# Cross-attention in a decoder layer: the first context block of the next batch is rounded two steps earlier

## The reference, cut to what matters

```
x = x + _L0_attn_ref(_layernorm(x), W_K, W_Q, W_V, W_O)
x = x + _L0_xattn_ref(_layernorm(x), ctx_2048, Wq, Wk, Wv)
x = x + _L0_ffn_ref(_layernorm(x), ...)          # mixture of experts

def _L0_xattn_ref(x, context, Wq, Wk, Wv):       # x (8,112,512), context (8,375,512)
    q = x @ Wq.T
    k_raw = context @ Wk.T
    v_raw = context @ Wv.T
    ...                                          # 32 heads of 16; k, v interleaved
    q = _rmsnorm(q); k = _rmsnorm(k)
    attn = softmax(q k^T * 0.25)
    return attn @ v
```

## Time and profile before

| | |
|---|---|
| median of 3 runs | 905.11 us (905.03 to 905.36) |
| the profiled execution | 905.82 us, its span 904.0 us |
| PE busy | 887.2 us |
| DVE busy | 599.0 us |
| ACT busy | 464.1 us |
| POOL busy | 203.5 us |

### The profile page before, as it was taken

The page is one execution under the profiler, slowest core; times in us unless marked ns, Lnnn a source line. Parts: engine busy times, 40 slices in busy tenths (PEclk is TensorE's granted clock), DMA queues, the critical chain, the costliest instruction groups (busy, mean ns, idle before and its releaser), DMA issues.

```text
span 904.0 us, 17919 instructions
## 1 busy us (share of the span) xinstructions
PE 887.2 (98%) x7088; PEld 777.9 (86%) x7088; DVE 599.0 (66%) x1304; ACT 464.1 (51%) x1119; POOL 203.5 (23%) x147
## 2 busy tenths in 40 slices
PE   8999999999999999999999999999999999999995
PEld 8998989898989898777787787777877898999994
DVE  7886575757575635765655655646557878888883
ACT  5533334343434344647666667566675336656551
POOL 0143232333333225201101101011000621132233
PEclk9999999999999999999999999999999999999998
DMA  6221232323212115140101001000043687989973
GB/s 225 64 94 41 91 126 94 123 94 123 95 53 96 40 47 180 35 129 30 55 12 36 14 24 36 13 24 14 1 147 140 230 310 295 364 280 308 294 203 46
DMA packets 42195, 104.56 MB, mean 116 GB/s; under 512 B 8208, under 2 KB 18560, under 8 KB 40192
## 3 DMA queue, kind: packets, MB, share of 16 engines
q1 hardware_dynamic: 37808, 94.23, 30.5%
q0 software_dynamic: 4304, 9.19, 5.0%
HBM read 75.57 MB, written 18.65 MB: 104 GB/s over the span
## 4 chain that ended last, share of the span: by engine, by line
PE 90%; DVE 2%; ACT 2%; POOL 2%; DMA 2%; issue 1%; SPq 0%; DVEq 0%
PE bank L595 23%; PE bank L596 23%; PE bank L597 23%; PE bank L852 5%; PE bank L869 5%; PE bank L695 3%; PE bank L671 2%; DMA ctx_f<-ctx 1%; PE bank L711 1%; PE bank L812 1%; PE bank L683 1%; PE bank L981 1%; PE bank L879 1%; POOL wkv_lo L2330 1%; PE bank L989 1%
## 5 line engine op out<-in xcount | busy, mean ns | idle before, releaser
L1380 ACT ACTIVATE ee<-bank 125x448 f32<-125x448 f32 x192 | 90.8, 546 | 15.0 <-PE bank L852 15.0
L1628 DVE TENSOR_TENSOR E_lo<-F,E_hi 128x940 fp32r<-128x940 f32 (+3 forms) x62 | 80.9, 1321 | 2.0 <-ACT E_hi L1147 1.9
L595 PE MATMUL bank<-wkv_hi,ctx_hi 128*125 128x512 f32 x192 | 79.9, 416 | 0.4 <-DVE kn L1905 0.4
L2330 POOL TENSOR_TENSOR ctx_lo<-ctx_f,ctx_hi 128x500 fp32r<-128x500 f32 x24 | 30.5, 1275 | 209.0 <-ACT ctx_hi L1147 209.0
L596 PE MATMUL bank<-wkv_hi,ctx_lo 128*125 128x512 f32 x192 | 76.1, 396 | 0.0
L597 PE MATMUL bank<-wkv_lo,ctx_hi 128*125 128x512 f32 x192 | 75.7, 394 | 0.0
L1147 ACT ACTIVATE E_hi<-F 128x940 fp32r<-128x940 f32 (+3 forms) x62 | 67.9, 1140 | 7.4 <-PE bank L597 3.6
L2330 POOL TENSOR_TENSOR wqk_lo<-wqk_f,wqk_hi 128x1024 fp32r<-128x1024 f32 x14 | 35.1, 2505 | 155.1 <-ACT wqk_hi L1147 155.1
L2440 POOL DMA_INDIRECT out<-yg,meta x21 | 39.1, 1864 | 127.7 <-DMA out<-yg,meta 71.7
L595 PE MATMUL bank<-wv_hi,xT_hi 128*128 128x256 f32 x224 | 63.4, 283 | 0.1
L597 PE MATMUL bank<-wv_lo,xT_hi 128*128 128x256 f32 x224 | 62.6, 279 | 0.0
(11 more groups left out here) (411 smaller groups left out, 2581.1 us busy)
## 6 DMA issues: line engine op xcount, KB each, us to landing
F<-wexp SPq DMA_DIRECT2D x14, 1408.0 KB, 7.6
F<-wexp SPq DMA_DIRECT2D x14, 768.0 KB, 6.9
wqk_f<-wqk SPq DMA_DIRECT2D x16, 512.0 KB, 4.3
ctx_f<-ctx SPq DMA_DIRECT2D x24, 250.0 KB, 2.7
slots<-zt SPq DMA_DIRECT2D x3, 1799.0 KB, 8.1
xg<-slots SPq DMA_DIRECT2D x21, 256.0 KB, 7.2
wv_f<-wv SPq DMA_DIRECT2D x8, 512.0 KB, 5.7
wo_f<-wo SPq DMA_DIRECT2D x8, 512.0 KB, 3.4
```

The lines of the kernel that those rows point to most:

```text
L595: e.matmul(out, a[0], b[0], start=first, stop=False)
L1380: e.activation(ee[(4 * n + r) % 8][:, :], SX[r][0:MS, 0:4 * T], ACT.Exp, scale=0.25).then_inc(*x_exped.did((n, r)))
L1628: return e.tensor_tensor(out, src, high.bitcast(F32), ALU.subtract)
L2330: return e.tensor_tensor(out, src, high.bitcast(F32), ALU.subtract)
```

## The change

The steps in which context blocks are rounded are 6b - 1, 6b + 2 and 6b + 3 instead of 6b + 1, 6b + 2 and 6b + 3. Block 3b + 3 is thus rounded in the last item's step of the batch before, for b = 1 to 6; the other blocks stay where they were. The high half on ACT, the low half on POOL and with it the release of a later load move.

```
-        ctx_step = {6 * b + i + 1: [3 * b + 3 + i] for b in range(NB - 1) for i in range(3) if b or i}
+        ctx_step = {6 * b + (-1, 2, 3)[i]: [3 * b + 3 + i] for b in range(NB - 1) for i in range(3) if b or i}
```

## The result

| | before | after |
|---|---|---|
| median | 905.28 us (15 runs, 904.78 to 907.33) | 907.73 us (15 runs, 906.45 to 909.58) |
| the profiled execution | 905.82 us, span 904.0 | 907.50 us, span 905.7 |

The ratio is 1.0026, interval 1.0018 to 1.0034: the changed kernel is slower by 2.45 us, where 4.9 us less were forecast. The time lies 5.8 us above the upper end of the range, 901.9.

The account below looks back on a forecast made before the run. PE (TensorE) was taken to bound the kernel, busy 98% of the span, with six stalls for kT. Removing them wins 4.95 us, other parts costing nothing: 905.11 - 4.95 = 900.2 us, range 899.5 to 901.9.

Parts of the forecast that it names:

- the six waits for kT: Cross-attention, line 711: PE waits 3.4 us in all for DVE's kT copy, late behind xn; the change removes them.
- Points 2 and 3: Third item's steps: xn falls from 1.43 to 0.55, the kT wait goes, steps last 6.19; 4.95 us won over six.
- Point 4: Step 6b - 1: ACT's added 0.60 us rounding fits its 1.26 us idle before copy oo, so costs nothing.
- Point 5: Step 6b - 1: POOL's low half costs DVE nothing; statistics at most 0.6 late against 0.77 idle; SE_lo could collide once.
- Point 6: Loads of the moved blocks: needed 13 us later than before the move at 571.2, landed by 557.7; cost nothing.
- The slower rival: Step 6b - 1: POOL holds DVE's kT copy or statistics 1.25 us, six times, 7.5 against 4.95: 907.7; chance 0.03.

Follow-up runs that it names:

- the kernel with block 6 ahead of the weights: The changed kernel, with SP still waiting for SE_lo of step 5 but then loading block 6 before the second shared-expert weight piece: 905.44 us, ratio 1.0001.
- the queue mended: The changed kernel, with the load of the second shared-expert weight piece put behind the load of block 7: 900.36 us, and 900.38 us when run again.

## Why the prediction was wrong

- What bounds the kernel, and the six waits for kT: right. They went, all six.
- Points 2 and 3, the gain of a third-item step: right. An unstalled step was put at 6.19 and measured 6.19 to 6.25; the sum was 4.95 and is 4.86. The missing 0.09 lies in steps of 6.20 and one of 6.25 (batch 3, which has 6.18 in the kernel with block 6 ahead of the weights). The last batch of the kernel before shows the 6.19 directly. A kernel in which nothing else happens (the queue mended) takes 900.36 and 900.38, forecast 900.2.
- Point 4, ACT in the last item's step: right in that a rounding costs nothing there, wrong in detail. In batch 1 the idle time before oo fell from 1.26 to 0.89, not to 0.7; part of it was taken where ACT waits for PE ahead of the squares.
- Point 5, DVE under POOL's new place: right, and the statistics that the trace of before couldn't show are not held at all.
- **Point 6, the loads, is the step that failed.** It named the release of the buffer by POOL as the only condition of a load, took the issue time of block 18 in batch 5 (555.02), found 13 us to spare, and let it stand for all six blocks. For blocks 9 to 21 it does: with these five moved there is no wait for a load and the time is 901.59. For block 6 the load stands in SP's queue behind `sf_load(1)`, which waits for step 5. Its issue at 426.85 was in the trace of before, as was SP's wait of 28.4 us at line 2559; both could be read there. For this block the 13 us to spare were minus 6: ACT stood 5.95 us at the rounding, and the load left after the rounding was due. "Cost nothing" measured 7.12 us.
- The slower rival gave 907.7, near the measured 907.73, by chance: its mechanism (POOL holding DVE in the new place) didn't occur, and the loss is one of 7 us in one step, not six of 1.25. The rival that was missing is a single wait for a load, with the clock's answer to the stop: 4.76 us of waiting cost 7.12.

What stays open: why POOL was 2 us later ahead of the cross-attention in one profiled execution of the mended kernel. How the runs of the kernel after and of the one with 2.72 us of stop come to scatter over 3 to 4 us was not tried either; the lowest mean clocks go mostly with the longer times.

## What to carry to other kernels

Before a step is moved ahead, look for the data of every instance of it, not of a typical one: the first and the last pass of a loop share their queues with work from the stage before, and a load that waits in an in-order queue behind somebody else's wait is late however early its own buffer was free. The queue engine's own waits (here one of 28.4 us) are where that is seen, and they look harmless as long as nobody needs what stands behind them. And a stop of TensorE should be priced with what follows it: here a half again on top of the stop.

## What the runs showed of the hardware

A one-column operation of DVE with both inputs in SBUF took 1.24 us instead of 0.16 when a POOL subtraction had begun 0.03 us before, in six of six steps; a layer norm's TENSOR_SCALAR (112x512) was held 0.88 us by one that had begun 0.10 before. Statistics over 112x512 from SBUF (0.68) and a copy from PSUM (0.41) under the same subtraction kept their length. A stop of PE of 4.76 us was followed by some 5 us at a granted clock of 0.50, and one of 2.72 us by 3.3 us at 0.50, which began when PE had been busy again for 1.2 us; they cost 2.36 and 1.57 us on top.
